# Attention output projection per head, from the unnormalised output: scaled by 1/row sum at the residual add, score bias moved to ScalarE

## The chip, the cores and the metric

One Trainium2 chip, one core. The metric is the device time of one execution in microseconds (us), the median of the runs.

## The reference, cut to what matters

The kernel computes two transformer layers on a sequence of 1024 tokens with 256 channels. Only the attention of the first layer is touched:

```python
q = (x @ Wq.T).reshape(b, t, 16, 128).transpose(0, 2, 1, 3)     # 16 query heads
k = (x @ Wk.T).reshape(b, t, 4, 128).transpose(0, 2, 1, 3)      # 4 key/value heads
v = (x @ Wv.T).reshape(b, t, 4, 128).transpose(0, 2, 1, 3)
q, k = _qknorm(q, q_scale), _qknorm(k, k_scale)
scores = einsum('bhtd,bhsd->bhts', q, repeat(k, 4)) / sqrt(128)
attn = softmax(where(causal, scores, min), axis=-1)
out = einsum('bhts,bhsd->bhtd', attn, repeat(v, 4))
return out.transpose(0, 2, 1, 3).reshape(b, t, 16 * 128) @ Wo.T
...
x = x + ga * attention(layernorm(x) * (1 + ca) + sa)
```

After it come a mixture of experts (64 experts), a state-space layer and a second mixture of experts. They are the same in both kernels.

## The kernel before, in words

**The loop.** Attention is one software pipeline, the same list of steps written out for every engine: `for n in range(FIRST, LAST)`. The 16 heads are worked in 4 groups `g` (one key/value head, 4 query heads each), and each group in two phases: `c = 0` has queries 0 to 511, which see keys 0 to 511 at most, and `c = 1` queries 512 to 1023, which see up to 1024 keys. A phase holds 4 heads, so there are 8 phases and 32 "heads" `m = n // 4` (a head of one phase), each of 4 steps; a step `n` is one block of 128 queries, `qi = n % 4`. `LAST` lets the pipeline run out after the 128 steps. A step of a `c = 0` phase has score rows of 128 to 512 keys, one of a `c = 1` phase 640 to 1024.

**One head along the pipeline.** In step n TensorE (PE in the profile) multiplies queries by keys (`scores`, three fp32r matmuls for each product, since every operand is split in a high and a low part, helper `three`, lines 1203 to 1205) into one of two pairs of PSUM banks. VectorE (DVE) takes the row maximum (`row_bias`, line 855) and makes the bias `negb` = -max * rqs (line 860); ScalarE (ACT) makes exp (`softmax_step`, line 585), with the row sum as a by-product. Mostly two steps later PE transposes the probabilities in groups of up to 4 blocks (line 1301, kind "p"), ACT copies the high part `pT_hi` out (line 574), DVE subtracts it to get `pT_lo` (line 869). In steps 4m+6, 4m+7 and 4m+8 PE weighs the values with them (`weigh_values`, pieces r = 0, 1, 2) into the one bank `PV_BANK`. The result there is not yet divided by the row sums.

**What follows for the head, before.** DVE makes `rinv` = 1/row sum, one column for each query block (line 922, step 4m+6). Queries lie along the free dimension of the output but along partitions in `rinv`, so in step 4m+8 PE transposes `rinv`, broadcast to 128 columns, four times (kind "r", line 1367), and ACT copies the spread rows to SBUF (`r_sb`, line 622). In step 4m+9 DVE multiplies the output by them (`o_f`, line 913; it stands behind that step's row maximum and bias, in front of its `pT_lo`), ACT copies the high part (`oT_hi`, line 647), GpSimd (POOL) subtracts for the low part (`oT_lo`, line 444). When all four heads of a phase are there, PE multiplies them by the output weights (`output_rows`, kind "y"): two groups of 24 matmuls, in steps 16p+23 and 16p+24 for phase p, that is in steps 7 and 8 of the next phase. DVE adds each to the residual `x` (line 901, 128x512).

**The banks.** Kinds p, r, y and the projections of the next half group (kv, q, qt, kt: `projection_at`) share three PSUM banks in turn. `bank_plan` writes out the order; a thing may be written when the thing three places earlier has been read out (`bank_free`), and PE works strictly in order, as every engine does. The next half group's projections lie in steps 0 to 6 of a `c = 0` phase (with kt at step 11) and in steps 0 to 9 of a `c = 1` phase (kt at 14). Five steps of a phase also have a part of the norm of queries and keys (`norm_part`) on DVE. Phase 7 has no projections.

**The end.** At step 129 DVE takes row statistics of the first four token tiles; after the last addition (`y_added`) it normalises, PE transposes and the expert layer starts.

## Time and profile before

| | us |
|---|---|
| median of 3 runs | 924.02 (919.67 to 925.37) |
| the profiled execution | 921.18 |
| its span | 919.4 |
| attention loop, first exp to the last addition | 51.6 to 509.9 |
| PE busy | 790.6 (86%) |
| DVE busy | 565.3 (61%) |
| ACT busy | 418.9 (46%) |
| POOL busy | 192.8 (21%) |

The profile is of one execution; its own time is 2.8 us below the median. "Busy" is the time in which an engine has an instruction in flight. Matmuls overlap, so what one costs PE is read from the distance between the starts of neighbours, not from its duration.

### The profile page before, as it was taken

The numbers are of one execution on the slowest core, as the hardware profiler recorded it, in microseconds if no ns is written. First come the engines' busy times: TensorE is split into PE (matmuls) and PEld (weight loads), VectorE is DVE, ScalarE is ACT, GpSimd is POOL, SyncE is SP. The second block draws the span as 40 slices with busy tenths as digits, with TensorE's granted clock in tenths as the row PEclk, the third lists the DMA queues.
The fourth block names the chain that finished last, engine by engine and source line by source line (L and its number), as shares of the span: only waits on it lengthen the run. The fifth ranks groups of instructions, "written<-read, shape, count | busy, mean of one in ns | idle before, by whom it ended". The sixth has DMA issues, their size and how long they took to land.

```text
span 919.4 us, 13272 instructions
## 1 busy us (share of the span) xinstructions
PE 790.6 (86%) x4582; PEld 646.2 (70%) x4582; DVE 565.3 (61%) x1317; ACT 418.9 (46%) x929; POOL 192.8 (21%) x145
## 2 busy tenths in 40 slices
PE   3787999989999899998998687999995347999992
PEld 3666788877888778887897566888884144666661
DVE  5647758677586775867766584656668962333333
ACT  3456757657577574775754312333332012333320
POOL 1005201142010430102301111332320103333310
PEclk9979999999999999999999688999997657999997
DMA  5000000100001000000000713333305311111104
GB/s 183 1 6 30 2 1 1 35 24 1 1 1 35 24 2 1 1 1 24 2 1 1 289 52 125 122 101 113 113 35 228 137 47 46 38 43 43 46 11 137
DMA packets 16752, 48.37 MB, mean 53 GB/s; under 512 B 2445, under 2 KB 7950, under 8 KB 15536
## 3 DMA queue, kind: packets, MB, share of 16 engines
q1 hardware_dynamic: 13440, 41.37, 12.9%
q0 software_dynamic: 2208, 5.12, 1.9%
q10 hardware_dynamic: 1040, 1.05, 0.4%
q8 instruction: 38, 0.62, 0.3%
q14 instruction: 26, 0.21, 0.1%
HBM read 43.07 MB, written 5.37 MB: 53 GB/s over the span
## 4 chain that ended last, share of the span: by engine, by line
PE 76%; DVE 14%; DMA 3%; ACT 3%; issue 2%; POOL 0%; SPq 0%; DVEq 0%; POOLq 0%; ACTq 0%
PE ps L1203 16%; PE ps L1204 16%; PE ps L1205 15%; PE ps L1527 9%; PE ps L1301 5%; PE ps L1545 4%; DVE mx L855 2%; DVE pT_lo L869 1%; PE ps L1367 1%; DVE stat L770 1%; PE ps L1213 1%; PE ps L1379 1%; PE ps L1537 1%; PE ps L1354 1%; DMA wbc<-combine 1%
## 5 line engine op out<-in xcount | busy, mean ns | idle before, releaser
L585 ACT ACTIVATE prob<-ps,negb,rqs 128x128 f32<-128x128 f32 (+7 forms) x128 | 106.7, 833 | 67.5 <-DVE negb L860 66.6
L574 ACT ACTIVATE pT_hi<-ps 128x512 fp32r<-128x512 f32 (+1 forms) x192 | 88.8, 491 | 64.5 <-PE ps L1301 58.2
L855 DVE TENSOR_REDUCE mx<-ps 128x1 f32<-128x128 f32 (+7 forms) x128 | 96.4, 753 | 26.1 <-PE ps L1293 24.6
L869 DVE TENSOR_TENSOR pT_lo<-ps,pT_hi 128x512 fp32r<-128x512 f32 (+1 forms) x192 | 99.8, 547 | 1.9 <-ACT pT_hi L574 1.8
L444 POOL TENSOR_TENSOR oT_lo<-o_f,oT_hi 128x512 fp32r<-128x512 f32 x32 | 41.3, 1290 | 281.8 <-ACT oT_hi L647 281.8
L1527 PE MATMUL ps<-wgu,xgT 128*128 x184 | 88.6, 605 | 1.0 <-ACT xgT L717 1.0
L1301 PE MATMUL ps<-ident,prob 128*128 128x128 f32 x576 | 86.1, 276 | 0.7 <-DVE qT_lo L889 0.4
L1203 PE MATMUL ps<-pT_hi,v_hi 128*128 128x512 f32 x192 | 72.9, 380 | 13.4 <-DVE pT_lo L869 13.4
L1203 PE MATMUL ps<-kT_hi,qT_hi 128*128 128x512 f32 (+1 forms) x192 | 70.0, 364 | 5.4 <-ACT prob L585 3.6
L1204 PE MATMUL ps<-kT_lo,qT_hi 128*128 128x512 f32 (+1 forms) x192 | 66.7, 347 | 0.0
L1205 PE MATMUL ps<-kT_hi,qT_lo 128*128 128x512 f32 (+1 forms) x192 | 66.5, 346 | 0.0
L1205 PE MATMUL ps<-pT_hi,v_lo 128*128 128x512 f32 x192 | 66.3, 345 | 0.0
L1204 PE MATMUL ps<-pT_lo,v_hi 128*128 128x512 f32 x192 | 66.2, 345 | 0.0
L1301 PEld LDWEIGHTS ps<-ident,prob 128*128 128x128 f32 x576 | 61.7, 141 | 2.6 <-DVE v_lo L878 0.9
L1203 PE MATMUL ps<-hT_hi,w_hi 128*128 128x512 f32 x136 | 55.6, 409 | 0.0
L734 ACT ACTIVATE th<-ps 128x512 f32<-128x512 f32 x23 | 13.7, 597 | 91.6 <-PE ps L1527 91.6
L1204 PE MATMUL ps<-hT_lo,w_hi 128*128 128x512 f32 x136 | 54.8, 403 | 0.0
L1205 PE MATMUL ps<-hT_hi,w_lo 128*128 128x512 f32 x136 | 54.5, 401 | 0.0
L960 DVE SCALAR_TENSOR_TENSOR fa<-th,ps 128x512 f32<-128x512 f32 x34 | 23.3, 685 | 49.2 <-ACT th L667 49.2
L667 ACT ACTIVATE th<-ps 128x512 f32<-128x512 f32 x34 | 20.3, 597 | 71.5 <-PE ps L1205 71.5
L1203 PE MATMUL ps<-wqkv_hi,hT_hi 128*128 128x512 f32 (+1 forms) x128 | 48.1, 376 | 5.0 <-DVE pT_lo L869 3.5
L1527 PEld LDWEIGHTS ps<-wgu,xgT 128*128 128x128 f32 x184 | 33.8, 195 | 25.7 <-issue 24.6
(255 smaller groups left out, 1971.0 us busy)
## 6 DMA issues: line engine op xcount, KB each, us to landing
wbc<-combine SPq DMA_DIRECT2D x16, 512.0 KB
wgu<-in_gate_up SPq DMA_DIRECT2D x8, 1024.0 KB, 12.3
w_raw<-in_ffn SPq DMA_DIRECT2D x17, 384.0 KB, 8.9
wdn<-in_down SPq DMA_DIRECT2D x1, 4096.0 KB, 17.4
wqkv_raw<-in_w_attn SPq DMA_DIRECT2D x4, 768.0 KB, 4.2
wo_raw<-in_w_out SPq DMA_DIRECT2D x4, 512.0 KB, 3.3
x<-in_x ACTq DMA_DIRECT2D x1, 1024.0 KB, 7.0
wmod<-in_wmod SPq DMA_DIRECT2D x1, 1024.0 KB, 9.8
```

Of the source, the lines that this page charges most:

```text
L444: nc.gpsimd.tensor_tensor(oT_lo[:, m % HPG, :], o_f[:], oT_hi[:, m % HPG, :], ALU.subtract).then_inc(oT_lo_done, 1)
L574: nc.scalar.activation(pT_hi[:, unit % NUNITS, 0:nb, qi * P:(qi + 1) * P], ps[:, ROTATING[place % 3], 0:nb * P].rearrange("p (j t) -> p j ...
L585: nc.scalar.activation(prob[:, n % 3, 0:w], ps[:, pair:pair + 2, :].rearrange("p b k -> p (b k)")[:, 0:w], ACT.Exp, bias=negb[:, n % 2:n % ...
L855: nc.vector.reduce_max(mx[:, i:i + 1], ps[:, pair:pair + 2, :].rearrange("p b k -> p (b k)")[:, 0:w], AX.X).then_inc(row_max, 1)
L869: nc.vector.tensor_tensor(pT_lo[dst], ps[:, ROTATING[place % 3], 0:nb * P].rearrange("p (j t) -> p j t", j=nb), pT_hi[dst], ALU.subtract). ...
L960: nc.vector.scalar_tensor_tensor(fa[:, hf, :], th[:, hf, :], 1.0, ps[:, 4 + 2 * hf, :], ALU.add, ALU.mult).then_inc(silu_done, 1)
L1203: nc.tensor.matmul(out, w_hi_, m_hi, start=start, stop=False, skip_group_check=True)
L1204: nc.tensor.matmul(out, w_hi_, m_lo, start=False, stop=False, skip_group_check=True)
L1205: return nc.tensor.matmul(out, w_lo_, m_hi, start=False, stop=stop, skip_group_check=True)
L1301: ins = nc.tensor.transpose(ps[:, ROTATING[place % 3], j * P:(j + 1) * P], prob[:, k % 3, (j0 + j) * P:(j0 + j + 1) * P], ident[:])
L1527: ins = nc.tensor.matmul(ps[:, bank, :], xgT[:, b % 2, kc, :], wgu[:, bass.ds(e, 1), c:c + H1].rearrange("p a c -> p (a c)"), start=(kc == ...
L1545: ins = nc.tensor.matmul(ps[:, 2 + b % 2, 0:D], hidT[:, b % 2, c, :], wdn[:, bass.ds(e, 1), c, :].rearrange("p a d -> p (a d)"), start=(c ...
```

## The change

- Kind "r" goes: no transposes of `rinv`, no `r_sb`, no `o_f`. `rinv` is made in step 4m+4.
- In step 4m+8 ACT copies the high part of the unnormalised output straight from `PV_BANK`, behind that step's exp and projection copies; DVE, at the end of its step 4m+8, subtracts it from the bank to get `oT_lo`. POOL has no part in it.
- Output rows are made head by head, in steps 4m+10 and 4m+11: 12 matmuls a head in two groups ("y", 64 groups of 6 matmuls in place of 16 of 24). DVE adds each 128x256 half of a group to `x` with the scale `rinv` as a per-partition scalar, two instructions a group.
- The bias: the row maximum is taken negated, and ACT multiplies it by `rqs` (a 128x1 copy with a scale from memory), waits for itself, and makes the exp.
- Output weights have two buffers, and POOL prepares group 0's before the loop and group g+1's during group g; the load of the next ones waits accordingly.

```diff
@@ -41,11 +41,12 @@
 STEPS = HEADS * 4
 PHASE = 4 * HPG
 PVLAG = 6
-RLAG = 8
-OLAG = 9
-YLAG = 23
+RLAG = 6
+OLAG = 8
+YLAG = 10
 FIRST = -12
-LAST = STEPS - PHASE + YLAG + 2
+LAST = STEPS - 4 + YLAG + 2
+Y_ADDS = 2 * HEADS
...
@@ -132,13 +133,10 @@
             whole_head[m] = groups
         for kind, index in projection_at(n):
             take(kind, index)
-        m = head_at(n, RLAG)
-        if m is not None:
-            take("r", m)
         for half in range(2):
-            p, r = divmod(n - YLAG - half, PHASE)
-            if r == 0 and 0 <= p < PHASES:
-                take("y", 2 * p + half)
+            m = head_at(n, YLAG + half)
+            if m is not None:
+                take("y", 2 * m + half)
     return order, at, needed, first_unit, whole_head
 
...
         wqkv_hi = weights("wqkv_hi", [P, KC, QKV], F32R)
-        wo_hi = weights("wo_hi", [P, HPG, D], F32R)
+        wo_hi = weights("wo_hi", [P, 2, HPG, D], F32R)
         (wqkv_raw,) = stage(("wqkv_raw", [P, KC, QKV], F32))
         (wqkv_lo,) = stage(("wqkv_lo", [P, KC, QKV], F32R))
         weights("under_wqkv", [P, KC, QKV])
-        (wo_raw,) = stage(("wo_raw", [P, HPG, D], F32))
-        (wo_lo,) = stage(("wo_lo", [P, HPG, D], F32R))
-        weights("under_wo", [P, HPG, D])
+        (wo_raw,) = stage(("wo_raw", [P, 2, HPG, D], F32))
+        (wo_lo,) = stage(("wo_lo", [P, 2, HPG, D], F32R))
+        weights("under_wo", [P, 2, HPG, D])
...
         (qT_hi, qT_lo, kT_hi, kT_lo, v_hi, v_lo, prob, pT_hi, pT_lo, oT_hi, oT_lo, q_f, k_f, sq, sqk,
-         r_sb, o_f, mx, negb, rsum, rinv, rqs) = stage(
...
-            ("oT_hi", [P, HPG, 512], F32R), ("oT_lo", [P, HPG, 512], F32R),
+            ("oT_hi", [P, 2, 512], F32R), ("oT_lo", [P, 2, 512], F32R),
             ("q_f", [P, 2, HPG * HD], F32), ("k_f", [P, 4, HD], F32),
-            ("sq", [P, HPG * HD], F32), ("sqk", [P, HD], F32), ("r_sb", [P, 2, 512], F32), ("o_f", [P, 512], F32),
...
@@ -353,14 +352,14 @@
             sp.dma_start(qks[:], qk_scale_d).then_inc(setup_loaded, 16)
             sp.dma_start(wqkv_raw[:], w_attn_d[0]).then_inc(wqkv_raw_in, 16)
             sp.dma_start(wmod[:, :, 2 * D:], wmod_d[:, 0, :, 2 * D:]).then_inc(rest_mod_loaded, 16)
-            sp.dma_start(wo_raw[:], w_out_d[0]).then_inc(wo_raw_in, 16)
-            for g in range(NG):
-                if g < NG - 1:
-                    sp.wait_ge(projected, g * NT + NT)
-                    sp.dma_start(wqkv_raw[:], w_attn_d[g + 1]).then_inc(wqkv_raw_in, 16)
+            sp.dma_start(wo_raw[:, 0, :, :], w_out_d[0]).then_inc(wo_raw_in, 16)
+            for g in range(NG - 1):
+                sp.wait_ge(projected, g * NT + NT)
+                sp.dma_start(wqkv_raw[:], w_attn_d[g + 1]).then_inc(wqkv_raw_in, 16)
+                sp.wait_ge(wo_ready, g + 1)
                 if g > 0:
-                    sp.wait_ge(wo_done, g * 4)
-                    sp.dma_start(wo_raw[:], w_out_d[g]).then_inc(wo_raw_in, 16)
+                    sp.wait_ge(wo_done, Y_ADDS // NG * g)
+                sp.dma_start(wo_raw[:, (g + 1) % 2, :, :], w_out_d[g + 1]).then_inc(wo_raw_in, 16)
...
@@ -439,11 +438,6 @@
                 nc.gpsimd.tensor_tensor(lo, raw, hi, ALU.subtract).then_inc(ready, 1)
 
 
-            def outputs_low(m):
-                pool.wait_ge(oT_hi_done, m + 1)
-                nc.gpsimd.tensor_tensor(oT_lo[:, m % HPG, :], o_f[:], oT_hi[:, m % HPG, :],
-                                        ALU.subtract).then_inc(oT_lo_done, 1)
-
             def normalise_keys(half):
                 pool.wait_ge(keys_copied, 4 * half + 4)
                 pool.wait_ge(qk_norm_step, half * NORM_STEPS + NORM_STEPS - 1)
...
             def output_weights(g):
+                raw = wo_raw[:, g % 2, :, :]
                 pool.wait_ge(wo_raw_in, 16 * g + 16)
-                nc.gpsimd.tensor_tensor(wo_raw[:], wo_raw[:], gates[:, 0:1, :].to_broadcast([P, HPG, D]),
+                nc.gpsimd.tensor_tensor(raw, raw, gates[:, 0:1, :].to_broadcast([P, HPG, D]),
                                         ALU.mult).then_inc(wo_scaled, 1)
                 pool.wait_ge(wo_scaled, g + 1)
-                split(wo_raw[:], wo_hi[:], wo_lo[:], wo_raw_in, 16 * g + 16, wo_high, g + 1, wo_ready)
+                split(raw, wo_hi[:, g % 2, :, :], wo_lo[:, g % 2, :, :], wo_raw_in, 16 * g + 16, wo_high, g + 1,
+                      wo_ready)
 
             pool.wait_ge(wqkv_high, 1)
             pool.wait_ge(ln_normed, NT)
             nc.gpsimd.tensor_tensor(wqkv_lo[:], wqkv_raw[:], wqkv_hi[:], ALU.subtract).then_inc(wqkv_ready, 1)
             normalise_keys(0)
+            pool.wait_ge(gates0_ready, 1)
+            output_weights(0)
             for g in range(NG):
-                for m in range(2 * HPG * g - 2, 2 * HPG * g):
-                    if m >= 0:
-                        outputs_low(m)
                 normalise_keys(2 * g + 1)
-                outputs_low(2 * HPG * g)
                 if g < NG - 1:
                     split(wqkv_raw[:], wqkv_hi[:], wqkv_lo[:], wqkv_raw_in, 16 * g + 32, wqkv_high, g + 2, wqkv_ready)
-                outputs_low(2 * HPG * g + 1)
-                output_weights(g)
-                for m in range(2 * HPG * g + 2, 2 * HPG * g + 5):
-                    outputs_low(m)
-                if g < NG - 1:
+                    output_weights(g + 1)
                     normalise_keys(2 * g + 2)
-                outputs_low(2 * HPG * g + 5)
-            outputs_low(HEADS - 2)
-            outputs_low(HEADS - 1)
...
-                act.wait_ge(bias_ready, n + 1)
+                i = n % 2
+                act.wait_ge(row_max, n + 1)
+                nc.scalar.activation(negb[:, i:i + 1], mx[:, i:i + 1], ACT.Copy,
+                                     scale=rqs[:, 4 * c + qi, h:h + 1]).then_inc(bias_ready, 1)
                 if n >= 3:
                     act.wait_ge(p_transposed, STEP_TRANSPOSED[n - 3])
+                act.wait_ge(bias_ready, n + 1)
                 nc.scalar.activation(prob[:, n % 3, 0:w],
                                      ps[:, pair:pair + 2, :].rearrange("p b k -> p (b k)")[:, 0:w], ACT.Exp,
                                      bias=negb[:, n % 2:n % 2 + 1], scale=rqs[:, 4 * c + qi, h:h + 1],
...
-            def spread_sums(m, bank):
-                act.wait_ge(r_spread, m + 1)
+            def outputs_high(m):
+                act.wait_ge(pv_done, NP * (m + 1))
                 if m >= 2:
-                    act.wait_ge(o_normed, m - 1)
-                nc.scalar.activation(r_sb[:, m % 2, :], ps[:, bank, :], ACT.Copy).then_inc(r_copied, 1)
+                    act.wait_ge(wo_done, 2 * (m - 1))
+                nc.scalar.activation(oT_hi[:, m % 2, :], ps[:, PV_BANK, :], ACT.Copy).then_inc(oT_hi_done, 1)
...
                 m = head_at(n, OLAG)
                 if m is not None:
-                    act.wait_ge(o_normed, m + 1)
-                    if m >= HPG and m % HPG == 0:
-                        act.wait_ge(wo_done, 2 * (m // HPG))
-                    nc.scalar.activation(oT_hi[:, m % HPG, :], o_f[:], ACT.Copy).then_inc(oT_hi_done, 1)
+                    outputs_high(m)
...
             signed_gates(grow[:], gsgn[:], gmag[:], 0)
+            nc.vector.memset(idle[:], 0.0).then_inc(gates0_ready, 1)
...
                 i = n % 2
                 dve.wait_ge(scored, n + 1)
                 nc.vector.reduce_max(mx[:, i:i + 1], ps[:, pair:pair + 2, :].rearrange("p b k -> p (b k)")[:, 0:w],
-                                     AX.X).then_inc(row_max, 1)
-                dve.wait_ge(row_max, n + 1)
-                if n >= 2:
-                    dve.wait_ge(exp_done, n - 1)
-                nc.vector.tensor_scalar(negb[:, i:i + 1], mx[:, i:i + 1], rqs[:, 4 * c + qi, h:h + 1], -1.0,
-                                        ALU.mult, ALU.mult).then_inc(bias_ready, 1)
...
             def add_output(y, bank):
                 dve.wait_ge(wo_done, y + 1)
-                t0 = 2 * (y % 4)
-                nc.vector.tensor_tensor(x[:, t0:t0 + 2, :], x[:, t0:t0 + 2, :],
-                                        ps[:, bank, :].rearrange("p (r d) -> p r d", r=2), ALU.add).then_inc(y_added, 1)
+                m, half = divmod(y, 2)
+                for r in range(2):
+                    qi = 2 * half + r
+                    t = 4 * ((m // HPG) % 2) + qi
+                    ins = nc.vector.scalar_tensor_tensor(x[:, t, :], ps[:, bank, r * D:(r + 1) * D],
+                                                         rinv[:, m % 2, qi:qi + 1], x[:, t, :], ALU.mult, ALU.add)
+                ins.then_inc(y_added, 1)
 
             for n in range(FIRST, LAST):
                 if 0 <= n < STEPS:
                     row_bias(n)
-                m = head_at(n, OLAG)
-                if m is not None:
-                    dve.wait_ge(pv_done, NP * (m + 1))
-                    dve.wait_ge(r_copied, m + 1)
-                    if m >= 1:
-                        dve.wait_ge(oT_lo_done, m)
-                    nc.vector.tensor_tensor(o_f[:], ps[:, PV_BANK, :], r_sb[:, m % 2, :], ALU.mult).then_inc(o_normed, 1)
                 for kind, index, detail, place in BANK_AT[n]:
                     if kind == "p":
                         probs_low(index, detail, place)
@@ -918,7 +897,7 @@
                 if m is not None:
                     dve.wait_ge(exp_done, 4 * m + 4)
                     if m >= 2:
-                        dve.wait_ge(r_spread, m - 1)
+                        dve.wait_ge(y_added, 2 * (m - 1))
                     nc.vector.reciprocal(rinv[:, m % 2, :], rsum[:, m % 2, :]).then_inc(row_inv, 1)
                 for kind, index, detail, place in BANK_AT[n]:
                     bank = ROTATING[place % 3]
@@ -932,11 +911,16 @@
                         keys_low(index, bank)
                     elif kind == "y":
                         add_output(index, bank)
+                m = head_at(n, OLAG)
+                if m is not None:
+                    dve.wait_ge(oT_hi_done, m + 1)
+                    nc.vector.tensor_tensor(oT_lo[:, m % 2, :], ps[:, PV_BANK, :], oT_hi[:, m % 2, :],
+                                            ALU.subtract).then_inc(oT_lo_done, 1)
                 chain = norm_part_at(n)
                 if chain is not None:
                     norm_part(*chain)
                 if n == STEPS + 1:
-                    dve.wait_ge(y_added, 4 * NG - 2)
+                    dve.wait_ge(y_added, Y_ADDS - 2 * HPG)
                     row_stats(lambda t: x[:, t, :], range(4), link)
...
                 kind, index = BANK_ORDER[place - 3]
                 if kind == "p":
                     pe.wait_ge(pT_lo_done, index + 1)
-                elif kind == "r":
-                    pe.wait_ge(r_copied, index + 1)
                 elif kind == "y":
                     pe.wait_ge(y_added, index + 1)
                 elif kind == "kv":
@@ -1306,7 +1288,7 @@
                 g, c = m // (2 * HPG), (m // HPG) % 2
                 pe.wait_ge(pT_lo_done, FIRST_UNIT[m] if r == 0 else WHOLE_HEAD[m])
                 if r == 0 and m >= 1:
-                    pe.wait_ge(o_normed, m)
+                    pe.wait_ge(oT_lo_done, m)
                 for j in PIECES[c][r]:
                     q0 = max(0, j - 4 * c) * P
                     u = (UNIT_BASE[m] + j // 4) % NUNITS
@@ -1316,14 +1298,15 @@
...
             def output_rows(y, bank):
-                g, p = y // 4, y // 2
-                pe.wait_ge(wo_ready, g + 1)
-                for h in range(HPG):
-                    pe.wait_ge(oT_lo_done, HPG * p + h + 1)
-                    for t in range(2):
-                        tok = slice((2 * (y % 2) + t) * P, (2 * (y % 2) + t + 1) * P)
-                        ins = three(ps[:, bank, t * D:(t + 1) * D], oT_hi[:, h, tok], oT_lo[:, h, tok],
-                                    wo_hi[:, h, :], wo_lo[:, h, :], h == 0 and t == 0, h == HPG - 1)
+                m, half = divmod(y, 2)
+                g, h = m // (2 * HPG), m % HPG
+                if m % (2 * HPG) == 0:
+                    pe.wait_ge(wo_ready, g + 1)
+                pe.wait_ge(oT_lo_done, m + 1)
+                for t in range(2):
+                    tok = slice((2 * half + t) * P, (2 * half + t + 1) * P)
+                    ins = three(ps[:, bank, t * D:(t + 1) * D], oT_hi[:, m % 2, tok], oT_lo[:, m % 2, tok],
+                                wo_hi[:, g % 2, h, :], wo_lo[:, g % 2, h, :], t == 0, True)
                 ins.then_inc(wo_done, 1)
...
-                    elif kind == "r":
-                        bank_free(place)
-                        pe.wait_ge(row_inv, index + 1)
-                        for qi in range(4):
-                            ins = nc.tensor.transpose(ps[:, bank, qi * P:(qi + 1) * P],
-                                                      rinv[:, index % 2, qi:qi + 1].to_broadcast([P, P]), ident[:])
-                        ins.then_inc(r_spread, 1)
```

## Rows read from the trace of the kernel before

**Rows 1.** The page, part 1: busy time, share of the span, instructions of each engine.
```profile
PE 790.6 (86%) x4582; PEld 646.2 (70%) x4582; DVE 565.3 (61%) x1317; ACT 418.9 (46%) x929; POOL 192.8 (21%) x145
```

**Rows 2.** By stretch (phases 0, 4, 5): us; PE, PEld, DVE, ACT, POOL busy; PEclk, DMA.
```profile
51.60:93.00 41.40, 35.37 (x216) 28.74 (x216) 27.98 (x81) 27.40 (x77) 12.93 (x7) 0.95 0.06 20
...
275.80:324.10 48.30, 44.47 (x308) 38.62 (x307) 33.85 (x90) 30.68 (x84) 15.47 (x9) 1.00 0.09 28
324.10:391.40 67.30, 65.44 (x425) 56.57 (x424) 49.05 (x102) 44.82 (x97) 9.72 (x7) 1.00 0.00 1
```

**Rows 3.** PE's waits in phase 4 (c = 0): us in total, times, longest.
```profile
PE ps L1203 <- DVE pT_lo L869: 3.5, 4, 1.6
PE ps L1203 <- ACT prob L585: 0.4, 1, 0.4
```

**Rows 4.** PE's waits in phase 5 (c = 1).
```profile
PE ps L1203 <- DVE pT_lo L869: 1.2, 1, 1.2
PE ps L1354 <- DVE pT_lo L869: 0.6, 1, 0.6
```

**Rows 5.** The chain that ended last, 51.6 to 511 us, by line.
```profile
by line: PE ps L1203 22.3%; PE ps L1204 20.9%; PE ps L1205 20.8%; PE ps L1301 11.0%; DVE mx L855 3.5%; issue 3.0%; DVE pT_lo L869 2.8%; PE ps L1367 2.7%; PE ps L1354 1.9%; DVE o_f L913 1.8%; PE ps L1293 1.5%; DVE negb L860 0.7%; ACT sq L601
```

**Rows 6.** PE in order of time: spread of row sums, output rows, next scores.
```profile
304.81 0.62 PE L1367 MATMUL ps<-ident,rinv 128*128 128x128 f32 x4
305.18 0.36 PE L1203 MATMUL ps<-wo_hi,oT_hi 128*128 128x256 f32 x1
305.38 0.28 PE L1204 MATMUL ps<-wo_lo,oT_hi 128*128 128x256 f32 x1
...
308.13 0.28 PE L1203 MATMUL ps<-kT_hi,qT_hi 128*128 128x256 f32 x1
```

**Rows 7.** Groups of instructions by shape: busy us, mean ns, idle before.
```profile
L574 ACT ACTIVATE pT_hi<-ps 128x512 fp32r<-128x512 f32 x96 | 55.8, 599 | 47.6 <-PE ps L1301 46.2
L860 DVE TENSOR_SCALAR negb<-mx,rqs 128x1 f32<-128x1 f32 x128 | 27.4, 214 | 4.5
L609 ACT ACTIVATE qT_hi<-ps,qks 128x512 fp32r<-128x512 f32 x32 | 21.9, 685 | 0.2 <-PE ps L1354 0.2
L869 DVE TENSOR_TENSOR pT_lo<-ps,pT_hi 128x256 fp32r<-128x256 f32 x32 | 13.2, 414 | 0.0
L901 DVE TENSOR_TENSOR x<-x,ps 128x512 f32<-128x512 f32 x16 | 11.0, 686 | 29.2 <-PE ps L1205 29.2
L1194 DVE SCALAR_TENSOR_TENSOR x<-xn_b,wpair,x 128x256 f32<-128x256 f32 x8 | 3.3, 478 | 0.2
```

**Rows 8.** The same view for ACT alone: a 128x1 copy.
```profile
L539 ACT ACTIVATE row_id<-const 128x1 f32<-128x1 f32 x1 | 0.2, 187 | 0.0
```

**Rows 9.** DVE, ACT and PE in order of time, last head of phase 4.
```profile
316.69 0.21 DVE L860 TENSOR_SCALAR negb<-mx,rqs 128x1 f32<-128x1 f32 x1
316.82 0.54 DVE L869 TENSOR_TENSOR pT_lo<-ps,pT_hi 128x384 fp32r<-128x384 f32 x1
316.93 0.46 ACT L585 ACTIVATE prob<-ps,negb,rqs 128x128 f32<-128x128 f32 x1 [0.89 <-DVE negb L860]
317.28 0.41 DVE L855 TENSOR_REDUCE mx<-ps 128x1 f32<-128x256 f32 x1
317.38 0.59 ACT L622 ACTIVATE r_sb<-ps 128x512 f32<-128x512 f32 x1
...
318.06 0.69 DVE L913 TENSOR_TENSOR o_f<-ps,r_sb 128x512 f32<-128x512 f32 x1
...
318.67 0.68 DVE L869 TENSOR_TENSOR pT_lo<-ps,pT_hi 128x512 fp32r<-128x512 f32 x1
...
319.40 0.50 PE L1203 MATMUL ps<-pT_hi,v_hi 128*128 128x512 f32 x1 [0.89 <-DVE pT_lo L869]
```

**Rows 10.** All engines in order of time, the end of the attention loop.
```profile
504.00 1.26 POOL L444 TENSOR_TENSOR oT_lo<-o_f,oT_hi 128x512 fp32r<-128x512 f32 x1 [5.98 <-ACT oT_hi L647]
...
509.20 0.69 DVE L901 TENSOR_TENSOR x<-x,ps 128x512 f32<-128x512 f32 x1 [2.18 <-PE ps L1205]
```

14 lines of the change are left out of this document (8 added, 6 removed).

## The prediction

> **What bounds the kernel now.** I read the page first: PE is busy 86% of the span, the next engine 61% [rows 1]. A share over the whole span says little about one stage, so next the busy time by stretch. Attention falls into phases of two kinds. In a c = 1 phase PE is busy 65.4 of 67.3 us, in a c = 0 phase 44.5 of 48.3 us, and in phase 0 only 35.4 of 41.4 us [rows 2]; the clock is at full speed (1.00, the 2.4 GHz level) in phases 4 and 5. DVE is busy 73% and 70% of those two: second, and not far off. Then PE's waits: 3.9 us in the c = 0 phase [rows 3], 1.8 us in the c = 1 phase [rows 4], nearly all for DVE's pT_lo. The chain that ended last agrees: PE's matmuls fill most of it, and three things that the change removes are on it: the spread of the row sums, L1367, 2.7% of 459.4 us = 12.4 us; o_f 1.8% = 8.3 us; negb 0.7% = 3.2 us [rows 5]. So the loop is bound by PE's queue, and in c = 0 phases by the path from row maximum to pT_lo as well.
>
> **The change, part by part.**
>
> *The spread of the row sums goes from PE.* Four transposes start at 304.81 and the next matmul at 305.18: 0.37 us. That next one takes 0.20 us to its follower, where the 23 steps from 305.38 to 308.13 take 0.12 us each [rows 6], so leaving the transposes costs 0.08 more. A head costs PE 0.45 us, 32 heads 14.4 us; the chain's 12.4 us supports it. This is the change's whole saving on PE: the matmuls of the output rows remain 384 at 0.12 us = 46 us, in other places.
>
> *The output rows move.* Instead of two blocks of 24 matmuls (2.9 us each) a phase, each head gets two groups of 6 (0.72 us each). A block of 2.9 us let DVE and ACT catch up; a group of 0.72 us does so less. For a phase the sum is the same. At the end, 24 of the last 48 matmuls (2.9 us) come before the last head's values instead of behind them, but phase 0, which had none, gets 24: I call that even. Phase 0 has 6.0 us of PE idle [rows 2] to hide them, so it may be up to 2.9 us better. At the end POOL's subtraction of 1.26 us [rows 10] becomes one of DVE's, about half as long, while the copy in front of it no longer needs r_sb and o_f; half of the last groups' additions come later instead. Even, within 2 us.
>
> *DVE.* It loses 128 bias instructions of 214 ns [rows 7]; they hold its queue for 0.13 us (316.69 to 316.82 [rows 9]) and some 0.04 us of waiting for the maximum: -22 us. It loses o_f and gains oT_lo, both 128x512 out of PSUM: 0. It loses 16 additions of 0.6 us (686 ns, less the overlap) and gains 128 of 128x256 with a scale from memory: 414 ns for such a subtraction from PSUM, 478 ns for this very form from SBUF [rows 7]. Eight of the latter keep DVE busy 3.3 us, so 0.41 us each: 52 - 10 = +43 us. In all DVE gets 21 us more in 458, 5%, and stays below PE in the mean. What matters is where it lies: a pair of additions (0.82 us) stands in front of the row maximum of the next step, 64 times.
>
> The Trainium skill speaks against this split: "VectorE: DVE Perf Modes", in its section on the TRN2 errata, says that the fixed cost is paid by each instruction, advises tiles of 512 elements or more, and gives (N+151)/0.96 ns for an fp32 tensor_tensor: an estimate of 424 ns at N = 256. The trace agrees, with 414. By that figure without overlap the additions would be 54 us.
>
> *ACT.* It gains 128 copies of 128x1 with a scale from memory. A 128x1 copy without one took 187 ns [rows 8]; a scale from memory lengthens a 128x512 copy from 599 to 685 ns, by 86 [rows 7]. So some 0.27 us latency against DVE's 0.21, about 0.2 us of queue. Bounds: 0.19 and 0.36. From row maximum to exp there were 0.29 us (317.28 is when the next maximum starts; exp started 0.24 us behind negb, at 316.93 against 316.69 [rows 9]); now about 0.35. ACT loses r_sb (0.5 us of queue), so four steps cost it 0.3 us more a head. Cover: ACT is busy 64 to 67% of those phases [rows 2]. The latency is covered by two pairs of score banks.
>
> *The new wait.* This is the dear part. oT_lo stands at the end of DVE's step 4m+8 and waits for ACT's oT_hi, which stands behind that step's exp. Behind it in DVE's queue are the next row maximum and the pT_lo for which PE waits. Before, o_f waited there for nothing: ACT had r_sb ready. For a c = 0 head without projections, from the end of the first maximum R, each price from [rows 9]: before, negb 0.13, pT_lo of 3 blocks 0.46, maximum 0.45, negb 0.13 and a gap, o_f 0.6, pT_lo 0.68 = R + 2.5. Now bias and start of exp 0.35, exp 0.45 (316.93 to 317.38 [rows 9]), oT_hi 0.6, oT_lo 0.65, maximum 0.4, pT_lo 0.68 = R + 3.15. The pair of additions makes R itself up to 0.45 later than the scores allow. Against that PE has 0.45 us less to do. So PE's wait ahead of the next values grows by about 1.5 us in a head where DVE was on time, and to some 2.5 us in the last head of the phase, where kt already made DVE late (0.89 us of wait at 319.40 [rows 9]). The first head has projections on PE to hide it. I estimate 0.3 + 1.3 + 1.5 + 2.6 = 5.7 us of waits a c = 0 phase, in place of 3.9: +1.9 against 4 x 0.45 = 1.8 saved. **A c = 0 phase nets nothing.** Both ends: nothing is lost (waits stay at 3.9: -1.8 a phase), or every head pays 1.5 to 2.6 (+2 a phase).
>
> In a c = 1 head the first piece of the values alone is twelve matmuls of 512 columns, each some twice the 0.12 us of 256 columns [rows 6], and each step's scores have 640 columns or more, so PE has more in hand between the two points. The same path there gives the first pT_lo some 0.1 us behind PE. Nothing is lost and the 1.8 us are kept: 4 x 1.8 = 7.2. The wait of 1.2 us [rows 4] is a projection that needs a bank whose pT_lo stood behind o_f; with o_f gone from there it falls to about 0.6, in the three c = 1 phases with projections: -1.8.
>
> *The rest.* POOL loses 32 subtractions; nobody but the output rows waited for them. Its first output weights come ahead of the second key norm, which is due a phase later. The loads wait on SP for weights prepared a phase earlier, with nothing behind them that is due. One memset on DVE ahead of the loop: 0.1 us. A group y takes a bank in steps 2 and 3 where the spread took one in step 0: next to projections the bank's last reader can be late. Between 0 and +1 us in each of seven phases; the sum takes 0, since two groups of every step's work lie between, and the range takes the rest.
>
> **Sum:** -7.2 (spread, c = 1) - 1.8 (bank behind o_f) + 0.4 (c = 0: -7.2 + 7.6) + 0 (ends) = -8.6 us. The profiled 921.2 becomes 912.6; it lies 2.8 below the median of 924.0, so the forecast for the median is 915.4.
>
> **The rivals.**
> *PE's queue takes all (faster).* If DVE catches up between its late points, the 14.4 us come whole, and part of the old waits goes with the blocks of 24 and with negb and o_f out of the path (3.2 + 8.3 us on the chain [rows 5], half of which oT_lo puts back): -14 to -20, 904 to 910. For: DVE is idle 27 to 30% of a phase [rows 2]. Against: the old waits for pT_lo are there with that same idleness.
> *The in-order wait takes over (slower).* DVE stands behind oT_hi in every head, and pairs of additions add 0.8 in front of a maximum. In the 16 heads of c = 0 phases 1.5 + 0.8 - 0.45 = 1.85 us each, 30 us, less the 15.6 of old waits that it replaces, less 7.2 in c = 1: +7; with bank waits in seven phases +14: 931 to 938. It decides from the point where oT_lo ends more than about 1.6 us behind the first maximum, if nothing later in the head gives DVE slack. For: my R + 3.15. Against: in a c = 0 phase DVE's 33.9 us [rows 2] become 33.9 + 16 x 0.41 - 2 x 0.6 - 16 x 0.17 = 36.5 of 48, so it has slack to catch up in.
> *Many small instructions (the skill's rule).* If each of the 128 additions holds DVE its full 0.48 us [rows 7], a pair is 0.96, 0.14 more than taken: at most 9 us over 64 pairs, 924: no change. That is how the section on the errata in "VectorE: DVE Perf Modes" would have it; the trace's overlap (0.41) speaks against it.
>
> **How the numbers follow.** The forecast (911 to 921) 0.43, PE takes all 0.31, the in-order wait 0.13, full-length additions 0.08, and 0.05 for neither. The range 903 to 930 reaches over the first rival, and holds the lower part of the space in front of the second. A difference under 1% (9.2 us) can't be told from none. The forecast lies at that edge: 0.13 of its 0.43 fall below 914.8, so faster 0.44; slower, from 933.3, 0.10; the rest 0.46.
>
> **What would show it.** Right: no L1367; c = 1 phases near 65 us each, c = 0 phases unchanged near 48 us, PE's waits for pT_lo of 5 to 6 us there; oT_lo's wait for oT_hi high among DVE's waits; the 128x1 copies near 0.27 us, the additions near 0.48. Wrong: PE's waits in c = 0 phases under 4 us (first rival), or more than 2 us in c = 1 phases (second). The stretch behind the loop should keep its length; if the clock falls to its lower level elsewhere than before, the forecast is off for a reason that I haven't priced.

## The result and the profile after

The change made the kernel slower: 938.84 us (median of 4 runs, 934.68 to 943.64) against 921.85 (919.55 to 925.37) for the kernel before on the same chip, a ratio of 1.0209 with a 95% interval of 1.0155 to 1.0262. The forecast of 915.4 and its whole range, 903 to 930, lie below it. The profiled execution took 937.61 us, 16.4 more than the profiled one of before (921.18).

The page of the changed kernel, part 1, answers to [rows 1]:

```profile
PE 789.3 (84%) x4453; PEld 641.2 (69%) x4454; DVE 576.5 (62%) x1302; ACT 439.1 (47%) x1025; POOL 151.7 (16%) x113
```

By stretch, phases 0, 4, 5 and 6 (us; PE, PEld, DVE, ACT, POOL busy; PEclk, DMA), to be held against [rows 2]:

```profile
46.90:96.70 49.80, 42.79 (x233) 35.26 (x232) 28.78 (x73) 31.15 (x91) 15.90 (x7) 0.81 0.08 27
284.10:336.00 51.90, 43.52 (x289) 36.84 (x288) 34.89 (x88) 33.22 (x94) 13.85 (x6) 1.00 0.08 26
336.00:403.80 67.80, 63.95 (x411) 55.19 (x411) 50.02 (x101) 47.39 (x109) 1.04 (x1) 1.00 0.00 1
403.80:458.10 54.30, 46.61 (x287) 39.21 (x286) 35.24 (x88) 33.15 (x95) 1.04 (x1) 0.94 0.00 1
```

In phase 4 PE is busy 0.95 us less than before and the phase is 3.6 us longer, both at a clock of 1.00. In phase 5 PE is busy 1.5 us less and the phase is 0.5 longer. TensorE's busy time fell, if by less than the forecast 1.8 a phase; its idle time more than ate it.

The whole attention stretch, from the first exponential to the last addition, adds up so: phase 0 +8.4 us (41.4 to 49.8), phases 2 and 4 +3.6 each, phase 6 +6.0 (48.3 to 54.3), the four c = 1 phases together +0.9, the end behind the last exponential -3.1 (18.1 to 15.0): +19.4. The first exponential comes at 46.9 us instead of 51.6, which is not the change's doing: in the runs below it came at 47 or 52 us in variants of either kernel (46.8 in e16, a variant of before, 52.1 in e11, one of the changed kernel). A median of a few runs can carry part of these 5 us, so lengths of the loop alone, from the first exponential to the last addition of the profiled execution, are given below beside the medians where two are near: 458.3 us before, 477.7 changed. Behind the loop +1.7 (409.5 to 411.2). 19.4 - 4.7 + 1.7 = 16.4.

PE's waits in phase 4, against [rows 3] (us in total, times, longest):

```profile
PE ps L1187 <- DVE pT_lo L851: 4.3, 3, 1.8
PE ps L1187 <- ACT prob L576: 2.7, 3, 1.2
PE ps L1187 <- DVE qT_lo L871: 1.4, 2, 0.9
```

And in phase 5, against [rows 4]:

```profile
PE ps L1187 <- DVE pT_lo L851: 1.7, 2, 1.3
PE ps L1283 <- DVE v_lo L860: 1.0, 1, 1.0
PE ps L1283 <- DVE pT_lo L851: 0.7, 1, 0.7
PE ps L1337 <- DVE pT_lo L851: 0.4, 1, 0.4
```

3.9 us became 8.4, and 1.8 became 3.8. The waits for an exponential (the scores need its bank) and for qT_lo are of kinds that before hardly had; in phase 5 it is projections and transposes that wait for a bank which a low half on DVE has not emptied. The chain that ended last, by line, against [rows 5]: no spread and no o_f any more, but what stood in 3.0% of "issue" is 7.5%, the row maximum went from 3.5 to 6.2%, and exp, oT_lo, the additions, oT_hi and the bias hold 13% between them:

```profile
by line: PE ps L1187 17.9%; PE ps L1189 16.6%; PE ps L1188 16.5%; issue 7.5%; PE ps L1283 6.6%; DVE mx L842 6.2%; DVE pT_lo L851 3.5%; ACT prob L576 3.0%; DVE oT_lo L917 2.9%; DVE x L886 2.8%; ACT oT_hi L613 2.3%; ACT negb L571 2.0%; ACT pT
```

Groups by shape, against [rows 7] (busy us, mean ns of one, idle before): the prices of the single instructions.

```profile
L886 DVE SCALAR_TENSOR_TENSOR x<-ps,rinv,x 128x256 f32<-128x256 f32 x128 | 55.6, 477 | 20.4 <-PE ps L1189 20.2
L571 ACT ACTIVATE negb<-mx,rqs 128x1 f32<-128x1 f32 x127 | 37.4, 295 | 61.4 <-DVE mx L842 59.5
L917 DVE TENSOR_TENSOR oT_lo<-ps,oT_hi 128x512 fp32r<-128x512 f32 x32 | 22.1, 691 | 17.6 <-ACT oT_hi L613 17.6
```

The same place as [rows 9], in order of time:

```profile
324.23 0.23 PE L1275 MATMUL ps<-mask_b,ident_b 128*128 128x128 bf16 x1
...
324.83 0.75 DVE L877 SCALAR_TENSOR_TENSOR kT_lo<-ps,qks,kT_hi 128x512 fp32r<-128x512 f32 x1 [1.54 <-ACT kT_hi L606]
...
325.50 0.86 DVE L886 SCALAR_TENSOR_TENSOR x<-ps,rinv,x 128x256 f32<-128x256 f32 x2
...
325.74 0.61 PE L1283 MATMUL ps<-ident,prob 128*128 128x128 f32 x4
...
326.29 0.28 DVE L842 TENSOR_REDUCE mx<-ps 128x1 f32<-128x128 f32 x1
...
326.99 0.46 ACT L576 ACTIVATE prob<-ps,negb,rqs 128x128 f32<-128x128 f32 x1
...
327.44 0.59 ACT L613 ACTIVATE oT_hi<-ps 128x512 fp32r<-128x512 f32 x1
327.59 0.44 PE L1187 MATMUL ps<-kT_hi,qT_hi 128*128 128x384 f32 x1 [1.24 <-ACT prob L576]
...
328.06 0.69 DVE L917 TENSOR_TENSOR oT_lo<-ps,oT_hi 128x512 fp32r<-128x512 f32 x1 [0.94 <-ACT oT_hi L613]
...
328.49 1.90 POOL L434 TENSOR_TENSOR wo_hi<-wo_raw,one 128x1024 fp32r<-128x1024 f32 x1
...
328.66 0.41 DVE L842 TENSOR_REDUCE mx<-ps 128x1 f32<-128x256 f32 x1
...
328.99 0.68 DVE L851 TENSOR_TENSOR pT_lo<-ps,pT_hi 128x512 fp32r<-128x512 f32 x1
...
329.73 0.50 PE L1187 MATMUL ps<-pT_hi,v_hi 128*128 128x512 f32 x1 [1.17 <-DVE pT_lo L851]
```

This shows both new waits in one head. The scores of this step end with the mask's matmul (324.23 + 0.23 = 324.46). DVE takes their maximum only at 326.29, 1.8 us later. Most of that was there before too: kT_lo, which waits for ACT, stands in front, and in the kernel before the maximum came 1.6 us after its scores:

```profile
314.52 0.23 PE L1293 MATMUL ps<-mask_b,ident_b 128*128 128x128 bf16 x1
...
316.37 0.28 DVE L855 TENSOR_REDUCE mx<-ps 128x1 f32<-128x128 f32 x1
```

New is that the pair of additions behind kT_lo then holds DVE for another 0.79 us, from 325.50 to 326.29. The exponential is late with it, and the scores of two steps on, which need its bank, wait 1.24. Then DVE itself stands 0.94 us for oT_hi, and what is queued behind it, the next maximum and pT_lo, makes PE wait 1.17 us more.

### The profile page after: what moved, and what is told of

It reads as the page before. It is cut to its first block, busy times and chain, and to the rows that moved or that the text cites. A ratio compares the mean times of both kernels' runs of the same rounds, so it can differ in the third digit from the quotient of the medians.

```text
span 935.8 us, 12915 instructions
## 1 busy us (share of the span) xinstructions
PE 789.3 (84%) x4453; PEld 641.2 (69%) x4454; DVE 576.5 (62%) x1302; ACT 439.1 (47%) x1025; POOL 151.7 (16%) x113
## 4 chain that ended last, share of the span: by engine, by line
PE 64%; DVE 19%; ACT 8%; issue 5%; DMA 3%; POOL 0%; SPq 0%; ACTq 0%; DVEq 0%; POOLq 0%
PE ps L1187 14%; PE ps L1188 13%; PE ps L1189 13%; PE ps L1503 9%; PE ps L1521 4%; PE ps L1283 3%; DVE mx L842 3%; DVE pT_lo L851 2%; ACT prob L576 2%; DVE oT_lo L917 1%; DVE x L886 1%; DVE stat L756 1%; ACT oT_hi L613 1%; PE ps L1355 1%; PE ps L1513 1%
## 5 line engine op out<-in xcount | busy, mean ns | idle before, releaser
L561 ACT ACTIVATE pT_hi<-ps 128x512 fp32r<-128x512 f32 (+1 forms) x192 | 89.3, 491 | 66.2 <-PE ps L1283 54.3
L1187 PE MATMUL ps<-pT_hi,v_hi 128*128 128x512 f32 x192 | 73.9, 385 | 18.5 <-DVE pT_lo L851 18.3
L886 DVE SCALAR_TENSOR_TENSOR x<-ps,rinv,x 128x256 f32<-128x256 f32 x128 | 55.6, 477 | 20.4 <-PE ps L1189 20.2
L571 ACT ACTIVATE negb<-mx,rqs 128x1 f32<-128x1 f32 x128 | 37.7, 295 | 63.8 <-DVE mx L842 61.9
L444 POOL TENSOR_TENSOR k_f<-k_f,rs_y 128x512 f32<-128x512 f32 x8 | 8.3, 1042 | 363.4 <-DVE rs_y L830 363.4
```

The lines of the kernel that those rows point to most:

```text
L561: nc.scalar.activation(pT_hi[:, unit % NUNITS, 0:nb, qi * P:(qi + 1) * P], ps[:, ROTATING[place % 3], 0:nb * P].rearrange("p (j t) -> p j ...
L571: nc.scalar.activation(negb[:, i:i + 1], mx[:, i:i + 1], ACT.Copy, scale=rqs[:, 4 * c + qi, h:h + 1]).then_inc(bias_ready, 1)
L886: ins = nc.vector.scalar_tensor_tensor(x[:, t, :], ps[:, bank, r * D:(r + 1) * D], rinv[:, m % 2, qi:qi + 1], x[:, t, :], ALU.mult, ALU.add)
L1187: nc.tensor.matmul(out, w_hi_, m_hi, start=start, stop=False, skip_group_check=True)
```

## The experiments

The theories, as the expectations name them. A: the bias on ScalarE. B: oT_lo waiting in DVE's order for ACT's oT_hi. C: TensorE's clock. D: the additions in front of a row maximum. E, later called the place theory: the place of the output matmuls in TensorE's order. The order theory is B and D together. "Place" is the step in which TensorE makes the output rows; "c = 0 phases of 52.8" means from the first exponential of the phase to that of the next. Every run was timed beside the kernel before; the phase lengths come from the profiled executions.

### Bias and low half, each alone and both

Bias back on DVE (the lines of the kernel before), in the changed kernel:

> The changed kernel with one part undone: the bias is again made by DVE right behind the row maximum (its 128x1 multiply, 0.21 us), not by ACT. Theory A, the in-order bias: in the changed kernel ACT's 128x1 copy takes 0.295 us and exp starts 0.39 us behind the start of that copy, so 128 steps hold ACT's queue for 50 us and everything behind it (exp, pT_hi, oT_hi) is late; then this comes down from 939 us to 920 to 926, c = 0 phases from 51.9 to about 48. Theory B, the in-order wait: DVE stands behind ACT's oT_hi at the end of step 4m+8 and the additions stand in front of row maxima; then this stays at 935 to 941. Theory C, the clock: the 34 us at its lower level in the loop come from shorter bursts of PE; then phases 0 and 6 keep their 50 and 54 us whatever engine makes the bias.

Bias on ScalarE, in the kernel before:

> The kernel before with this one part alone: row maximum taken negated, bias by ACT's 128x1 copy. Theory A: slower by about the 10 to 17 us that the change costs, 932 to 939. Theory B: ACT has slack here, 0.1 us more from row maximum to exp is covered by two pairs of score banks: 921 to 926.

oT_lo one step later, behind that step's probabilities:

```diff
+                m = head_at(n, OLAG + 1)      # behind probs_low, ahead of the reciprocal
+                if m is not None:
+                    dve.wait_ge(oT_hi_done, m + 1)
+                    nc.vector.tensor_tensor(oT_lo ...)
...
-                m = head_at(n, OLAG)          # at the end of the step
```

> The changed kernel with oT_lo's subtraction moved on DVE from the end of step 4m+8 to step 4m+9, behind that step's row maximum and pT_lo, so DVE never stands waiting for ACT's oT_hi in front of a row maximum. Theory B: down to 922 to 928, PE's waits for pT_lo in a c = 0 phase from 4.3 to about 2 us. Theory A: no more than 3 us better, 935 to 939.

> Both at once: bias on DVE, oT_lo in step 4m+9. If the two costs are separate, they add, and what is left is the saving on PE (14.4 us by the prediction's count): 905 to 914. If one hides the other, it ends within 3 us of the better of the two alone.

Measured, as ratios to before with their intervals: 1.0311 (1.0249 to 1.0373), 1.0013 (0.9976 to 1.0049), 1.0228 (1.0172 to 1.0284) and 1.0208 (1.0152 to 1.0264). The second settles A for the kernel before: the same 128 copies of 295 ns cost it nothing. In the changed kernel e1 does not settle it, since e1 met a disturbance of its own (below); its phases 0 and 6, 47.4 and 54.9 us, do not settle C either. Both changes at once (e4) are no better than the later low half alone. The later low half (e3) took the three c = 1 phases before the last from 67.8 to 65.9 us, the 1.9 that B asked for. But the total hardly moved, 939 to 937 (the loop, 477.7 to 473.4): phases 2 and 4 went from 51.9 at a clock of 1.00 to 54.0 at 0.91 and 52.8 at 0.97, phase 6 from 54.3 at 0.94 to 50.7 at 1.00. In phase 4 of e3 TensorE no longer waits 4.3 us for pT_lo but 4.4 for oT_lo, which now comes late for the next head's values. Phases 2 and 4 also met the disturbance described below, phase 6 did not.

### Additions, and rows per head with everything else as before

e5, the additions behind the next row maximum:

```diff
+                for kind, index, detail, place in BANK_AT.get(n - 1, []):   # behind row_bias(n)
+                    if kind == "y":
+                        add_output(index, ROTATING[place % 3])
...
-                    elif kind == "y":
-                        add_output(index, bank)
```

> The changed kernel, with each pair of additions to the residual moved on VectorE from the end of a step to the next step, right behind its row maximum. Theory D (the pair, 0.87 us in 64 steps, stands in front of the next row maximum, and so of the exponential on which the scores of two steps later wait): 924 to 931, with TensorE's waits for the exponential in a c=0 phase down from 2.7 us to about 0.5. Theory E (what costs is the place of the output matmuls: eight spread over each head instead of blocks of 24, with one PV bank and a clock that falls where TensorE has gaps): 935 to 941, as the changed kernel. If the low half of the output, now behind nothing, comes earlier in its step, it gives up to 2 us a c=0 phase back under either.

e6, `x[:, t, 0:1]` and one column of the bank in place of 256:

> The changed kernel, with each addition cut to the first of its 256 columns: the other 255 columns of the residual get no attention output. The waits, their order and TensorE's work stay. It prices the length of the additions: about 128 x 0.4 us of VectorE's time goes. Theory D: 922 to 930. Theory E: 933 to 940, since VectorE's load sets nothing. If it is well under 922, VectorE as a whole was short of time, and the old figure of 21 us more on it was not hidden.

e7, e5 with oT_lo in step 4m+9, ahead of the additions:

> The changed kernel with both moves on VectorE: the additions behind the next row maximum, and the low half of the output in step 4m+9 right behind the row maximum, ahead of the probabilities' low half, so that ACT's high half is done before VectorE comes to it and the PV bank comes free early. Theory D with the wait for the high half: 918 to 927. Theory E: 932 to 940.

e8, the changed kernel with r, r_sb, o_f, POOL's oT_lo, the bias on DVE and the plain 128x512 addition of the kernel before. Its output rows come two steps later, in 4m+12 and 4m+13, and it makes 64 such additions where before made 16 (its expectation says 32 more; it is 48):

> Output rows made and added per head as in the changed kernel, but from the output normalised as before: spread of the row sums on TensorE, its copy on ACT, the normalised output on VectorE, the low half on GpSimd, bias on VectorE, and one plain 128x512 addition in place of the scaled pair. So the place of the output matmuls is the only large difference to the kernel before. Theory E: 930 to 940. Theory D or the wait for the high half (both absent here): 915 to 924 plus up to 5 us for 32 more plain additions on VectorE.

Measured: e5 961.54 us, 1.045 (1.0394 to 1.0506), a clear miss; e6 932.28, 1.0113 (1.0043 to 1.0182); e7 940.45, 1.0244 (1.0158 to 1.033); e8 935.67, 1.0169 (1.0112 to 1.0225). e5 shows what the additions also do: they free a bank. In its c = 1 phases, 75.2 us long, PE waited for them:

```profile
PE ps L1284 <- DVE x L886: 6.0, 4, 1.6
```

So an addition is in the way of a maximum in front of it and in the way of a projection behind it. e6 says that the additions' length is worth some 7 us (938.8 to 932.3; its interval just overlaps that of the changed kernel; the loop, 477.7 to 470.2), less than half of the loss. e7, with c = 1 phases of 71.9 for the same reason as e5 (4.7 us of such waits in phase 5), had c = 0 phases of 50.4, 50.2 and 48.9: the best so far. e8 looked like proof of E, and I took it so. It was not; see "What hid the gain of the low half".

### Where TensorE makes the rows

e9, both groups of a head in step 4m+13, where no piece of the values stands (four reciprocals kept, and one more wait between additions, as in e10, e11, e12 and e14); e10, the same with e3's order; e11, all eight groups of a phase in steps 7 and 8 of the next phase again, four a step; e12, that with e3's order.

```diff
-YLAG = 10
+YLAG = 13
...
-            m = head_at(n, YLAG + half)
+            m = head_at(n, YLAG)
```

> The changed kernel, with both groups of a head's output rows three steps later and in one step (4m+13), the only one of four that has no piece of the values on TensorE; four buffers for the reciprocals of the row sums, so that nothing waits for that. Theory E (the place of the output matmuls in TensorE's order is the cost): the time moves, down if their being next to the pieces of the values is what costs, 925 to 932; if their spreading as such costs, it stays at 935 to 941. A theory in which the time is lost by VectorE's wait for ACT's high half or by the additions as such: 936 to 941.

> The same with the low half of the output one step later on VectorE too, behind the probabilities' low half, so that it doesn't wait for ACT. Theory E: 1 to 5 below the kernel with the place alone, as the c=1 phases keep the 1.9 us each that this move gave before, and values have longer until the PV bank is wanted: 921 to 930. Otherwise 934 to 940.

> The changed kernel with its unnormalised output, scaled additions, bias on ACT and no spread, but the output rows of a phase are made in two blocks again, at the steps of the kernel before (four groups of 6 matmuls in each of steps 7 and 8 of the next phase; high and low half of four heads and the reciprocals of eight kept). Theory E: 905 to 920, since the spread's 14.4 us are gone and the blocks are back; some 3 us of it may go to banks that wait for the additions, eight pairs of 0.87 in a row. If unnormalising and the wait for the high half are the cost: 930 to 942.

> The same blocks, and the low half of the output one step later on VectorE. Theory E: 900 to 917, a few us under the blocks alone if the wait for ACT's high half costs c=1 phases 1.9 us each as it did in the changed kernel. Otherwise 930 to 940.

Measured: 945.24 us, 1.0306 (1.0251 to 1.0361); 923.94, 1.0062 (1.0023 to 1.01); 933.66, 1.0139 (1.0089 to 1.019); 936.3, 1.0196 (1.0164 to 1.0229). E fails: with its blocks back and no spread, the kernel is 15 to 18 us slower than before, where E wanted it no slower, and the place alone (e9) makes it worse. Yet e9 and e10 differ in nothing but where DVE does oT_lo, and that is 21 us. Most of it lies in the c = 1 phases (70.3 in two of e9's, 66.6 in e10's): in phase 5 TensorE waits 4.7 us for pT_lo in e9 and 1.4 in e10. DVE's order decides, and how much it does depends on what TensorE has to do meanwhile.

### Is TensorE still the bound?

e15 and e16 leave out two of the three matmuls of each product of the output rows (high x low and low x high; the rows are coarser), 8 of 12 a head, in the changed kernel and in the one before. e13 and e14 choose DVE's order by kind of phase; e14 has e9's place too.

```diff
+def short(n):
+    return 0 <= n < STEPS and (n // PHASE) % 2 == 0
...
+                # behind row_bias(n): oT_lo of head_at(n, OLAG + 1) if short(n);
+                # then the additions of step n - 1 if short(n - 1)
+                # behind probs_low: oT_lo if not short(n); at the end: additions if not short(n)
```

> The changed kernel with VectorE's order chosen by kind of phase: in c=0 phases the low half of the output and the additions behind the next row maximum (as in e7, whose undisturbed c=0 phase took 48.9 us), in c=1 phases the low half behind the probabilities' low half and the additions in their old place (as in e3, whose c=1 phases took 65.9). If VectorE's order is what holds the c=0 phases: 49 and 66 us, 918 to 926. If it is the place of TensorE's work for the output rows: c=0 phases stay at 50.5 or more, 928 to 938.

> The same order, and both groups of output rows of a head in the step without values, as in e10 (923.9). If place and order add up: 910 to 920, which would be the first version that beats the kernel before. If they are the same cost seen twice: 921 to 930.

> The changed kernel with the output rows made from high x high alone: two of the three matmuls of each product are left out, 8 of 12 a head, 0.12 us each, 3.84 us a phase. Place theory: in c=0 phases without a low clock nearly all of it comes back (51.9 to about 48.5), as each group stands on the path; in c=1 phases all of it, too. Order theory: half or less of it comes back in c=0 phases.

> The kernel before with the same two of three matmuls left out, 32 of 48 a phase, 3.84 us too. Place theory: c=0 phases get little of it back, under 1.5 us of 48.3, since the two blocks fill a gap there, c=1 phases all. Order theory: as much comes back as in the changed kernel.

Measured: e13 922.81 us, 1.0037 (0.9999 to 1.0075); e14 913.99, 0.9946 (0.9911 to 0.9981); e15 925.91, 1.0074 (1.0034 to 1.0113); e16 893.46, 0.9716 (0.965 to 0.9782). The last two take 8 x 0.12 x 32 = 30.7 us of matmuls from each kernel. Before gave back 917.68 - 893.46 = 24.2 of it; the changed one 938.84 - 925.91 = 12.9. The place theory said the reverse. Phases 4 and 5 of e16, then of e15:

```profile
261.40:307.70 46.30, 41.42 (x275) 35.01 (x275) 33.76 (x90) 30.71 (x84) 15.48 (x9) 1.00 0.10 30
307.70:371.10 63.40, 61.54 (x393) 52.68 (x392) 48.91 (x102) 44.82 (x96) 9.73 (x7) 1.00 0.01 1
```

```profile
278.40:331.50 53.10, 44.90 (x257) 36.97 (x256) 35.14 (x88) 33.05 (x95) 13.81 (x6) 0.87 0.08 26
331.50:397.30 65.80, 60.53 (x379) 51.19 (x378) 49.46 (x101) 47.60 (x108) 1.04 (x1) 1.00 0.00 1
```

Of 3.84 us less work, a c = 1 phase of before returned 3.9 and a c = 0 phase 2.0; of the changed kernel 2.0 and -1.2, the clock of the latter down to 0.87. The c = 1 phases are the clean comparison, all at a clock of 1.00: there TensorE's queue is the bound in the kernel before, and in the changed one only about half of what it is spared comes back. In e15's c = 0 phases the idler TensorE also had the lower clock, so the total of 12.9 mixes two effects. And e14 is the first version that beats the kernel before, by 0.5% (the loop, 454.3 against 458.3).

### What hid the gain of the low half

e13's phases 4 and 6 differ in step 9, 4.1 against 1.9 us, and so do those of e14 (4.0 and 1.9). In that step, all engines in order of time, e14 has:

```profile
305.49 2.75 POOL L438 TENSOR_TENSOR wqkv_hi<-wqkv_raw,one 128x1536 fp32r<-128x1536 f32 x1
...
305.92 2.35 DVE L837 TENSOR_SCALAR rqs<-rs_y 128x16 f32<-128x16 f32 x1
...
308.30 0.56 DVE L846 TENSOR_REDUCE mx<-ps 128x1 f32<-128x384 f32 x1
```

It ends with POOL's copy of the weights, 305.49 + 2.75 = 308.24, and DVE's whole queue stands behind it. The same two in the changed kernel, phase 4:

```profile
319.61 0.24 DVE L833 TENSOR_SCALAR rqs<-rs_y 128x16 f32<-128x16 f32 x1
...
319.78 2.75 POOL L434 TENSOR_TENSOR wqkv_hi<-wqkv_raw,one 128x1536 fp32r<-128x1536 f32 x1
```

Which of them comes first is a matter of half a microsecond: there DVE starts 0.17 us ahead of POOL and takes 0.24 us, in e14 it starts 0.43 behind and takes 2.35. It is behind, and takes 1.5 to 2.4 us, in phases 0, 2 and 4 of e3, e4, e7, e12, e13, e14 and e18 (one of e10's, 1.55), 1.4 in two phases of e9, and 2.7 in all three of e1, enough for the 1% by which e1 is slower than the changed kernel (3 x 2.5 us; whether that is all of it, no run says). L837 does not meet a copy of weights in phase 6, where POOL has none to split. What follows on TensorE, in stretches of 2 us of the run of e14:

```profile
306.00:308.00 2.00, 1.83 (x9) 1.21 (x8) 2.00 (x1) 0.28 (x1) 2.00 (x1) 1.00 0.73 233
308.00:310.00 2.00, 0.30 (x3) 0.31 (x4) 1.97 (x6) 1.01 (x3) 1.92 (x2) 1.00 0.07 29
310.00:312.00 2.00, 2.00 (x15) 1.86 (x14) 1.55 (x5) 1.08 (x4) 2.00 (x2) 0.75 0.00 0
312.00:314.00 2.00, 2.00 (x12) 2.00 (x10) 0.88 (x3) 1.47 (x4) 2.00 (x1) 0.50 0.00 0
```

PE is busy 0.30 of 2 us, and behind it the granted clock is at 0.50, the 1.2 GHz level, for a while. It does not always follow: in phase 4 of the changed kernel TensorE was as idle, and the clock stayed at 1.00:

```profile
318.00:320.00 2.00, 0.25 (x1) 0.25 (x2) 1.86 (x8) 0.78 (x3) 1.22 (x2) 1.00 0.00 0
```

Phases 4 and 6 of e14, which have the same length in the kernel before (48.3 us):

```profile
273.00:321.90 48.90, 44.33 (x289) 38.33 (x289) 36.45 (x88) 32.91 (x94) 13.82 (x6) 0.97 0.09 28
388.50:435.10 46.60, 42.94 (x286) 36.72 (x286) 34.27 (x88) 32.91 (x95) 1.04 (x1) 1.00 0.00 1
```

So stall and clock together are 2.3 us in this phase; if phases 0 and 2 lose as much, e14 still has some 7 us to give, an estimate. In e13, whose phase 4 kept a clock of 1.00, the same two phases differ by only 0.9 (49.8 and 48.9). That moving either instruction away brings any of it was not tried. A rule of the Trainium skill, "SBUF — State Buffer", section "Who interferes with whom", names the kind: VectorE and GpSimd share a pair of ports; a VectorE instruction in a mode that uses both of its port pairs, open to a tensor_scalar, contends for it, whichever issues first holds it for its whole instruction, and the other fully blocks. The end of L837 on the end of POOL's instruction agrees; which mode L837 ran in, no row shows.

It also upsets the reading of e8. There two small instructions, both with their inputs in SBUF, met POOL's work on weights in each of the first three c = 1 phases:

```profile
376.77 2.40 POOL L459 TENSOR_TENSOR wo_raw<-wo_raw,gates 128x1024 f32<-128x1024 f32 x1
376.88 2.32 DVE L853 SCALAR_TENSOR_TENSOR rs_t<-rs_t,rs_in 128x20 f32<-128x20 f32 x1
...
381.25 2.39 POOL L442 TENSOR_TENSOR wo_lo<-wo_raw,wo_hi 128x1024 fp32r<-128x1024 f32 x1
381.39 2.29 DVE L852 TENSOR_TENSOR rs_t<-rs_y 128x20 f32<-128x20 f32 x1
```

Beyond their usual 0.18 and 0.17 that is 4.3 us, where the kernel before loses 1.1 in the same way (one of 1.23 us). So 3.2 of the 4.2 us by which e8's c = 1 phases are longer than those of before (71.5 and 67.3) can be this, if a stall of DVE is passed on in full; its c = 0 phases are 1.1 to 1.4 longer. Of the 18.3 us by which e8's loop is longer (476.6 against 458.3) that would be some 10, and leave some 8 for rows made per head with their 48 more additions. I argue this from the trace, and no run isolates it.

### Dividing the order's gain

e13 with only its additions moved, and with only its low half:

> The changed kernel with the additions behind the next row maximum in c=0 phases alone; the low half of the output stays at the end of its step and waits for ACT. If the additions ahead of a maximum cost by themselves: c=0 phases of 50 to 50.5 and 928 to 934. If it is the wait for ACT's high half: c=0 phases stay at 51.2 to 51.9, 935 to 940. c=1 phases stay at 67.8 under both.

> The changed kernel with the low half of the output one step later alone: right behind the row maximum in c=0 phases, behind the probabilities' low half in c=1 phases; the additions stay at the end of their step. If the wait is the cost: 50 and 65.9 us, 922 to 928, near the 922.8 of both parts. If the two need each other: 930 to 937, as in the kernel with the low half behind the probabilities everywhere (937.1).

Measured: 934.45 us, 1.0153 (1.0089 to 1.0218), and 929.21, 1.0102 (1.0063 to 1.0141). From 1.0209 the additions alone take 0.6 points (the intervals overlap, so this part is not shown), the low half alone 1.1, both 1.7, and e14's place another 0.9 on top. By the medians: 938.8, 934.5 or 929.2, 922.8, 914.0; by the loop: 477.7, 473.8 or 467.0, 460.0, 454.3.

The totals nearly add up, but phase by phase that can't be read, since the clock moved too. In phases 2 and 4 the changed kernel takes 51.9 us each, e17 51.8 each, e18 50.8 and 52.4, and e13 49.8 each. e17's phase 4, at a clock of 0.97 instead of 1.00:

```profile
283.00:334.80 51.80, 45.05 (x289) 37.97 (x288) 34.11 (x87) 33.13 (x95) 13.85 (x6) 0.97 0.08 26
```

PE is busy 1.5 us more there than in the changed kernel, and waits 1.6 us less (6.8 against 8.4), so that the phase hardly moves. Part of e17's gain lies in phases 0 and 6, where the clock differs as well; most of e18's is the 1.9 us of each c = 1 phase before the last. What each move does to PE's waits is plain. In e17's phase 4 the waits for an exponential are gone, and 1.1 us of waits for the additions came:

```profile
PE ps L1195 <- DVE pT_lo L855: 4.3, 3, 1.8
PE ps L1291 <- DVE x L890: 0.7, 1, 0.7
PE ps L1195 <- DVE x L890: 0.4, 1, 0.4
```

In e18's, the waits for pT_lo are shorter and those for an exponential are all there:

```profile
PE ps L1196 <- ACT prob L580: 2.8, 3, 1.3
PE ps L1196 <- DVE pT_lo L855: 2.6, 3, 1.0
```

So the additions in front of a maximum are what makes the exponential late, as theory D said, and oT_lo at the end of its step is a part of what makes pT_lo late, as B said.

## Why the prediction was wrong

**The failed steps are "A c = 0 phase nets nothing" and "Nothing is lost and the 1.8 us are kept" for c = 1 heads.** With the ends, which I called even, the first is off by 18.1 us and the second by 9.9: the loop got 19.4 us longer where I had it 8.6 shorter. I subtracted the spread from a queue that I took to stay the bound, and followed the new wait into one consumer alone, the values.

*c = 1 phases.* Forecast: -7.2 and -1.8 in all. Measured: +0.9. oT_lo in front of DVE's next work costs 1.9 a phase (e3 and e18: 65.9). The bank that I expected earlier, because o_f was gone, comes no earlier: oT_lo or a pair of additions stands where o_f stood, pT_lo is late behind it, and the waits rose from 1.8 to 3.8 where I had them fall to 1.2. 1.0 of the 3.8 is v_lo, for which DVE itself had waited 1.5 us for ACT.

*c = 0 phases.* Forecast: +0.4 over four. Measured: +13.2 in phases 2, 4 and 6, and +5.3 for phase 0 with the end. The path in the last head of the phase came out as I added it up: from R, the end of the first maximum, I had 3.15 us to the end of pT_lo, and the rows give 326.57 to 329.67, 3.10. (For the kernel before I had 2.5, and its rows give 316.65 to 319.35, 2.70; so the path grew by 0.40, not 0.65.) I had R itself late by up to 0.45 through the additions; in this head they hold it for 0.79. And I charged that lateness only to pT_lo. It also delays the exponential, for whose bank the scores two steps on wait: 2.7 us in phase 4, not in my sum, and gone in e17, which moves the additions. With qT_lo's 1.4, and pT_lo at 4.3, it makes the 8.4 us measured in place of my 5.7.

*Prices.* The scaled addition 477 ns and 0.87 a pair (I had 0.82), oT_lo 0.69 (0.65), the bias 0.295 (0.27) right. ACT's queue is held 0.39 us a step by the bias (326.60 to 326.99), not 0.2, and it cost nothing all the same (e2). The rule on many small instructions, a rival at 924, named the additions but for a reason that failed: it priced a pair at 0.96, and it is 0.87. What mattered was that a pair stands in front of a maximum, and e6, which shortens it to 0.34, gets back some 7 us.

*Ends and clock.* I called the ends even. Phase 0 took the 2.9 us of matmuls that the end gave back and 5.5 more, its mean clock 0.81 against 0.95. I did not price the clock, and said so. In phase 6, at 0.94, it accounts for 2.4 us: 54.3 against the 51.9 of phases 2 and 4, which are at 1.00. From the mean clocks, phase 0 was at the lower level for some 19 us (4 before) and phase 6 for some 6.5 (none before); e1's expectation says 34 in all, these rows give 25. At half speed 21 us more of it cost at most some 10 of the loop's 19.4, an estimate; what is left, the 7.2 of phases 2 and 4 above all, stands at a clock of 1.00.

*Rivals.* "The in-order wait takes over", 931 to 938 with a chance of 0.13, comes nearest. Its core is what happened: DVE stands behind oT_hi, and pairs of additions stand in front of a maximum. So did its sign, waits of more than 2 us in c = 1 phases (3.8). That 938.8 lies beside its range is in part luck: it kept the 7.2 us of the c = 1 phases, which were lost, and had neither the wait for the exponential's bank nor the clock. I set it low because DVE had slack on average (36.5 of 48 us); it was busy 34.9 of 51.9, and that slack never helped, as it lay where DVE was itself waiting for ACT or for scores.

*What stays open.* How much of phase 0's 5.5 us is the clock and how much the order; whether moving the additions alone is worth anything in the total; whether the bias on ACT costs anything in the changed kernel, where e1 was disturbed; and what e14 would do with the meeting of L837 and POOL out of the way.

## What to carry to other kernels

When work leaves the busiest engine, count the gain only after following each instruction that the change adds to a second engine's queue to every consumer of what stands behind it, here to the values, the scores' bank and the projections' bank. A way to measure who is the bound: take the same work out of both kernels, and see how much of it comes back (24.2 of 30.7 us, against 12.9), in stretches with the same clock (3.9 of 3.84 against 2.0). The right place in a queue can differ by stage: one order gave c = 0 phases of 49 us and c = 1 phases of 72, another 51 to 54 and 66, and with an order for each (e13) and the later place (e14) came the gain. What one move does is best read from the busiest engine's waits in one phase, beside the clock of that phase: in e17 1.6 us less of waiting was hidden by a clock of 0.97.

## What was unexpected of the hardware

A 128x16 VectorE instruction from SBUF to SBUF, 0.17 to 0.24 us by itself, took up to 2.7 us when it started behind a GpSimd instruction of 2.75 us on 128x1536, and in the case shown ended with it; two instructions on 128x20, 0.17 and 0.18 us by themselves, took 2.29 and 2.32 in the same way (e8). Maxima and subtractions that read PSUM ran beside GpSimd at their usual lengths (in the changed kernel 0.68 us for the 128x512 subtraction at 328.99, beside POOL's instruction of 328.49 to 330.39). TensorE's clock fell to 0.50 after a stretch in which TensorE was busy 0.30 of 2 us (e14), and in the changed kernel's phase 6 after one of 0.98 of 2 us, within phases in which it was busy 86% and more; yet in phase 4 of the changed kernel, after one of 0.25 of 2 us, it stayed at 1.00.
